# A decoder layer on one core: the self-attention stage rebuilt around stacked queries, two heads per score product and values in column quarters

## The reference

```python
x = x + self_attn(layernorm(x))      # 32 heads of 16, ONE key and value head shared by all
x = x + cross_attn(layernorm(x), ctx)# 32 heads of 128, 8 key/value heads, rotary positions, mask
x = x + ffn(layernorm(x))            # silu(x Wg) * (x Wu), then Wd; inner size 1376

# self_attn
q = (h @ Wq).reshape(b, s, 32, 16);  k, v = split(h @ Wkv)         # k, v: [b, s, 16]
scores = einsum("bqhd,bkd->bhqk", q, k) / 4 + slope[h] * (pos_k - pos_q)
attn = softmax(where(causal, scores, -inf));  out = einsum("bhqk,bkd->bqhd", attn, v) @ Wo
```

## Time and profile before

| | before |
|---|---|
| median of 3 runs | 1018.83 us (1015.87 to 1019.94) |
| profiled execution | 1015.36 us, of it 1013.5 us from the first to the last instruction (span) |
| TensorE busy | 985.4 us (97%) |
| VectorE, ScalarE, GpSimd busy | 589.1, 429.1, 382.0 us |
| granted TensorE clock, mean | 0.995 of full speed |
| self stage | from 0 to 234.5 us of the span |

### The profile page before, as it was taken

How to read it: one execution, slowest core, us unless ns; L and a number is a source line. 1 busy time by engine, 2 the same in 40 slices (tenths; PEclk the granted TensorE clock), 3 DMA queues, 4 the chain that set the end, 5 groups by cost and what they waited for, 6 DMA issues and landing times. The chain is left out here.

```text
span 1013.5 us, 15742 instructions
## 1 busy us (share of the span) xinstructions
PE 985.4 (97%) x5128; PEld 808.2 (80%) x5128; DVE 589.1 (58%) x973; ACT 429.1 (42%) x1239; POOL 382.0 (38%) x375
## 2 busy tenths in 40 slices
PE   5999999989999999999999999999999989999998
PEld 3877777877888888888888888888888768888787
DVE  3856566635776676666666767667666773343100
ACT  2777676751433533523533533533432543333100
POOL 6422222163652642652642633634623422222200
PEclk9999999989999999999999999999999999999999
DMA  6000000211120210210210200210300012122001
GB/s 202 13 11 11 11 10 10 63 52 52 32 63 11 55 50 0 72 31 0 72 31 0 72 31 0 73 30 11 82 1 0 33 32 68 67 71 74 10 32 42
DMA packets 41538, 40.17 MB, mean 40 GB/s; under 512 B 3104, under 2 KB 28832, under 8 KB 41504
## 3 DMA queue, kind: packets, MB, share of 16 engines
q1 hardware_dynamic: 41120, 38.68, 12.7%
q0 software_dynamic: 384, 1.05, 0.3%
HBM read 37.62 MB, written 2.10 MB: 39 GB/s over the span
## 5 line engine op out<-in xcount | busy, mean ns | idle before, releaser
L624 PE MATMUL bank<-cross_wo_hl,cross_outT_hl 128*128 128x512 f32 x768 | 191.7, 398 | 1.0 <-POOL cross_wo_hl L618 0.6
L624 PE MATMUL bank<-hsT_hl,cross_wqkv_hl 128*128 128x512 f32 x768 | 188.2, 394 | 0.0
L624 PEld LDWEIGHTS bank<-cross_wo_hl,cross_outT_hl 128*128 128x128 f32 x768 | 143.1, 188 | 35.5 <-POOL cross_wo_hl L618 1.6
L624 PEld LDWEIGHTS bank<-hsT_hl,cross_wqkv_hl 128*128 128x128 f32 x768 | 141.9, 188 | 29.3
L937 ACT ACTIVATE cross_scores<-cross_scores,cross_negmax 128x128 f32<-128x128 f32 x256 | 99.8, 391 | 127.1 <-DVE cross_negmax L875 127.1
L797 POOL TENSOR_TENSOR cross_qT<-rotated,rotated_other_half 128x512 f32<-128x512 f32 x64 | 82.8, 1293 | 161.9 <-DVE rotated_other_half L839 161.9
L624 PE MATMUL bank<-hsT_hl,ff_gate_upT_hl 128*128 128x512 f32 (+1 forms) x528 | 120.4, 390 | 2.7 <-DVE ff_gate_upT_hl L1139 2.7
L624 PEld LDWEIGHTS bank<-hsT_hl,ff_gate_upT_hl 128*128 128x128 f32 (+1 forms) x528 | 97.7, 185 | 25.0 <-DVE ff_gate_upT_hl L1139 3.1
L947 ACT CAST cross_outT_hl<-bank 128x512 fp32r<-128x512 f32 x64 | 37.1, 579 | 143.4 <-PE bank L624 142.5
L837 DVE TENSOR_TENSOR rotated<-bank,cosT 128x512 f32<-128x512 f32 x80 | 55.2, 690 | 71.4 <-PE bank L624 71.3
L624 PE MATMUL bank<-ctxT_hl,cross_wqkv_hl 128*128 128x512 f32 x384 | 94.3, 394 | 1.1 <-PEq L74 1.1
(11 more groups left out here) (117 smaller groups left out, 1535.6 us busy)
## 6 DMA issues: line engine op xcount, KB each, us to landing
staged_rows<-in_wq SPq DMA_DIRECT2D x32, 256.0 KB, 2.8
staged_rows<-in_wo SPq DMA_DIRECT2D x32, 256.0 KB, 2.7
staged_rows<-in_wg SPq DMA_DIRECT2D x11, 256.0 KB, 2.5
staged_rows<-in_wu SPq DMA_DIRECT2D x11, 256.0 KB, 2.6
staged_rows<-in_wd SPq DMA_DIRECT2D x11, 256.0 KB, 2.7
ctx_tok<-in_ctx SPq DMA_DIRECT2D x8, 256.0 KB, 2.6
staged_rows<-in_wk SPq DMA_DIRECT2D x8, 256.0 KB, 3.0
staged_rows<-in_wv SPq DMA_DIRECT2D x8, 256.0 KB, 3.0
```

Of the source, the lines that this page charges most:

```text
L624: i = nc.tensor.matmul(out, stationary[:, a], moving[:, b], start=(first and k == 0), stop=(last and k == 2))
```

## The change

Only the self stage, its constants and the layout of its inputs change; the cross stage and the feed-forward keep their instructions.

- Normalised rows are kept for four sequences at a time, transposed and split into high and low parts in `hsT` (which the cross stage uses later). Queries of four sequences are made at once, transposed from the start (512 columns are 4 x 128 tokens), with float32r products and split weights; so are keys and values. Four sequences are done before the first scores, four while sequences 2 and 3 run.
- `stack_queries` copies the queries of one sequence with 12 DMAs from SBUF to SBUF: for each of four groups of 32 rows (two heads), the high part goes to rows 0 to 31 and 32 to 63 of `qT`, the low part to rows 64 to 95. Rows 96 to 127 hold the slopes and slopes times positions, loaded once. `qT` has room for two sequences. `kexp` holds for all sequences, in the same rows, the high, low and high parts of the keys of two heads side by side, and positions. One score product then gives two heads with their bias: a step is two products of 256 columns, each started and ended by itself.
- VectorE adds only the causal mask (one 128 x 128 table). ScalarE exponentiates in place with the accumulator. VectorE takes the reciprocal of the row sums, GpSimd multiplies the probabilities by it.
- Values: after four steps (16 heads), four float32 products take 32 columns of a table with the values between zeros as the stationary operand and 512 columns of transposed probabilities as the moving one, and write the four 32-row quarters of one bank; a second group of four adds the other 16 heads. The result is already transposed for the output product, which is made with float32r products of split parts.
- The context comes in already transposed (laid out on the host) and is split by ScalarE and GpSimd in sequences 4 and 5. The rotary tables are gathered at the start and transposed in sequence 0.
- Side work uses three banks (`MB`), in an order that `before_attention` and `steps_in` write out.

```diff
+BANKS = 3
+SLOT_S = 4
+SLOT_PT = 6
+RINGS = 2
+GROUPS_OF_ROWS = ((0, 0), (1, 0), (2, 1))
+Q_DMAS = 16 * QUAD * len(GROUPS_OF_ROWS)
+def before_attention():
+    return ([("ln", c, (0,)) for c in range(HALF)] + [("q", c, (0, 1, 2, 3)) for c in range(HALF)]
+            + [("kv", 0, (0, 1, 2, 3)), ("vt", 0, (0,))])
+def steps_in(b, s):
+    front, back = (0, 1), (2, 3)
+    own = {
+        (0, 0): [("tab", 0, (0,))], (0, 1): [("tab", 1, (0,))], (0, 2): [("tab", 2, (0,))], (0, 3): [("tab", 3, (0,))],
+        (0, 4): [("ln", 4, (0,))], (0, 5): [("ln", 5, (0,))], (0, 6): [("ln", 6, (0,))], (0, 7): [("ln", 7, (0,))],
+        (1, 0): [("kv", 1, front)], (1, 1): [("kv", 1, back)], (1, 3): [("vt", 1, (0,))],
+        (2, 1): [("q", 4, front)], (2, 2): [("q", 4, back)], (2, 3): [("q", 5, front)], (2, 4): [("q", 5, back), ("ln", 8, (0,))],
+        (2, 7): [("q", 6, front)], (3, 0): [("q", 6, back)], (3, 1): [("q", 7, front)], (3, 2): [("q", 7, back)],
+    }.get((b, s), [])
+    if b >= 1 and s in (5, 6):
+        own = own + [("out", b - 1, front if s == 5 else back)]
+    if 3 <= b < SEQS and s == 3:
+        own = own + [("ln", SEQS + b - 2, (0,))]
+    return own
...
+            def load_q(b, quarters=range(QUAD)):
+                sp.wait_ge(sem["bank_read"], use_of("q", HALF * (b // HALF) + HALF - 1) + 1)
+                if b >= RINGS:
+                    sp.wait_ge(sem["scores1"], STEPS * (b - RINGS + 1))
+                for r in quarters:
+                    stack_queries(sp, sem, qT, q_hl, b, r)
...
+            def probs(n):
+                pool.wait_ge(sem["rinv1"], n + 1)
+                nc.gpsimd.tensor_tensor(S[:, n % SLOT_S], S[:, n % SLOT_S], rinv[:, n % SLOT_S, :].unsqueeze(2).to_broadcast([P, QUAD, P]),
+                                        ALU.mult).then_inc(sem["probs1"], 1)
...
+                    dve.wait_ge(sem["scores1"], n + 1)
+                    if n >= SLOT_S:
+                        dve.wait_ge(sem["probs_transposed1"], n - SLOT_S + 1)
+                    nc.vector.tensor_tensor(S[:, n % SLOT_S], SC[n % 2][:].rearrange("p (h k) -> p h k", h=QUAD),
+                                            causal[:].unsqueeze(1).to_broadcast([P, QUAD, P]), ALU.add).then_inc(sem["biased1"], 1)
+                    dve.wait_ge(sem["biased1"], n + 1)
+                    nc.vector.tensor_reduce(negmax[:, n % SLOT_S, :], S[:, n % SLOT_S], AX.X, ALU.max, negate=True).then_inc(sem["max1"], 1)
+                    if n >= 1:
+                        dve.wait_ge(sem["exp1"], n)
+                        nc.vector.reciprocal(rinv[:, (n - 1) % SLOT_S, :], rowsum[:, (n - 1) % SLOT_S, :]).then_inc(sem["rinv1"], 1)
+                    for kind, i in ended_in(b, s):
+                        read_bank(kind, i)
...
+                    for kind, i in ended_in(b, s):
+                        high(kind, i)
+                    if b >= 1 and s == 4:
+                        attnT_high(b - 1)
+                    if n >= 3:
+                        probsT(n - 3)
+                    act.wait_ge(sem["max1"], n + 1)
+                    for j in range(QUAD):
+                        e = nc.scalar.activation(S[:, n % SLOT_S, j, :], S[:, n % SLOT_S, j, :], ACT.Exp, bias=negmax[:, n % SLOT_S, j:j + 1],
+                                                 accum_out=rowsum[:, n % SLOT_S, j:j + 1])
+                    e.then_inc(sem["exp1"], 1)
...
+            def scores(n):
+                b, s = n // STEPS, n % STEPS
+                if s == 0:
+                    pe.wait_ge(sem[f"q_loaded{b % RINGS}"], Q_DMAS * (b // RINGS + 1))
...
+                if n >= 2:
+                    pe.wait_ge(sem["biased1"], n - 1)
+                for k in range(2):
+                    e = nc.tensor.matmul(SC[n % 2][:, k * 2 * P:(k + 1) * 2 * P], qT[:, b % RINGS, 2 * s + k, :], kexp[:, b, :], start=True, stop=True)
+                e.then_inc(sem["scores1"], 1)
+            def values(w):
+                b, second = w // 2, w % 2
+                pe.wait_ge(sem["probsT1"], QUAD * w + QUAD)
...
+                for j in range(QUAD):
+                    e = nc.tensor.matmul(OB[32 * j:32 * j + 32, :], v[:, b, 0:32] if second else v[:, b, 16:48],
+                                         PT[:, (QUAD * w + j) % SLOT_PT], start=not second, stop=bool(second))
+                e.then_inc(sem["pv1"], 1)
+            for kind, i, tiles in before_attention():
+                step(kind, i, tiles)
+            scores(0)
+            for b in range(SEQS):
                 for s in range(STEPS):
                     n = STEPS * b + s
+                    if n + 1 < STEPS * SEQS:
+                        scores(n + 1)
+                    if n >= 3:
+                        transposes(n - 3)
+                    if n >= 7 and n % QUAD == 3:
+                        values(n // QUAD - 1)
+                    for kind, i, tiles in steps_in(b, s):
+                        step(kind, i, tiles)
+            for n in range(STEPS * SEQS - 3, STEPS * SEQS):
+                transposes(n)
+            values(2 * SEQS - 1)
+            step("out", SEQS - 1, (0, 1, 2, 3))
+def stack_queries(queue, sem, qT, q_hl, b, r):
+    at = (b % HALF) * P
+    for group, part in GROUPS_OF_ROWS:
+        queue.dma_start(qT[32 * group:32 * group + 32, b % RINGS].rearrange("p (c r) k -> p c r k", r=QUAD)[:, :, r, :].bitcast(F32),
+                        q_hl[32 * r:32 * r + 32, part, :, at:at + P].bitcast(F32)).then_inc(sem[f"q_loaded{b % RINGS}"], 16)
```

More of the change, by code:

```diff
@@ new lines, in last_of, with bank_uses, use_of, highs_before @@
+def last_of(kind):
+    return 3 if kind in ("q", "kv", "out") else 0
+def bank_uses():
+    uses = [(kind, i) for kind, i, tiles in before_attention()]
+    for b in range(SEQS + 1):
+        for s in range(STEPS):
+            uses += [(kind, i) for kind, i, tiles in steps_in(b, s) if last_of(kind) in tiles]
+    return uses
+USES = bank_uses()
+def use_of(kind, i):
+    return USES.index((kind, i))
+def highs_before(u):
+    return sum(1 for kind, i in USES[:u] if kind != "out")
+def ended_in(b, s):
+    if s == 0:
+        b, s = b - 1, STEPS
+    return [(kind, i) for kind, i, tiles in steps_in(b, s - 1) if last_of(kind) in tiles] if b >= 0 else []
@@ new lines, in _ @@
+            load_q(0, (0, 1))
+            load_q(1)
+            load_q(2)
+            load_q(3)
+            load_ctx(0)
+            load_ctx(1)
+            load_q(4)
+            for j in range(2, 5):
+                load_ctx(j)
+            load_q(5)
+            for j in range(5, 8):
+                load_ctx(j)
+            for j in range(PIECES):
+                if j == 0:
+                    sp.wait_ge(sem["wo1_low"], QUAD)
+                if j == SLOTS:
+                    load_q(6)
+                    load_q(7)
@@ L279, in body @@
+            read_bank("ln", 3)
+            dve.wait_ge(sem["wkv1_high"], 1)
+            nc.vector.tensor_tensor(wkv_hl[:, 1], wkv[:], wkv_hl[:, 0].bitcast(F32), ALU.subtract).then_inc(sem["wkv1_low"], 1)
+            for c in range(HALF):
+                read_bank("q", c)
+            read_bank("kv", 0)
+            read_bank("vt", 0)
+            dve.wait_ge(sem["causal_loaded"], 16)
+            for b in range(SEQS):
                 for s in range(STEPS):
                     n = STEPS * b + s
-                    if s == 3 and since(b, 1):
-                        normalise(b - 1, 1)
@@ new lines, in _ @@
+            for t, done in ((0, "wq1_first"), (2, "wq1_second")):
+                act.dma_start(wq[:, t:t + 2, :], io["wq1"].rearrange("(t p) n -> p t n", p=P)[:, t:t + 2, :]).then_inc(sem[done], 16)
+            for t in range(KT):
+                if t % 2 == 0:
+                    high("ln", t)
+                    high("ln", t + 1)
+                act.wait_ge(sem["wq1_first" if t < 2 else "wq1_second"], 16)
+                nc.scalar.copy(wq_hl[:, 0, t, :], wq[:, t, :]).then_inc(sem["wq1_high"], 1)
@@ L375, in body @@
+            act.wait_ge(sem["wkv1_loaded"], 16)
+            nc.scalar.copy(wkv_hl[:, 0], wkv[:]).then_inc(sem["wkv1_high"], 1)
+            for c in range(HALF):
+                high("q", c)
+            act.wait_ge(sem["bank_read"], use_of("q", HALF - 1) + 1)
+            for r in (2, 3):
+                stack_queries(act, sem, qT, q_hl, 0, r)
+            high("kv", 0)
+            high("vt", 0)
+            for b in range(SEQS):
                 for s in range(STEPS):
                     n = STEPS * b + s
-                    if s == 1 and scores and since(b, 1):
-                        copy_qT(b, 1)
@@ L468, in hs_transposes @@
[L468 to L484 removed]
+                    i = nc.tensor.transpose(bank[:, t * width:(t + 1) * width], src[:, t * P:(t + 1) * P], ident[0:width, 0:width])
```

731 lines of the change are left out of this document (310 added, 421 removed).

## The result

The change made the kernel slower by about one per cent. It takes 1028.28 us (median of 4 runs, 1027.03 to 1029.58), against 1017.35 us for the kernel before on the same chip (4 runs): a ratio of 1.0106, 95% interval 1.0076 to 1.0135. The forecast was 1000 us, with a range of 985 to 1018, and 0.12 for slower. The profiled execution took 1027.03 us, its span 1024.9 us.

A forecast was written before the change was run, and what follows sets the result against it. TensorE alone was taken to bound the self stage, ScalarE after the change. 40.2 + 158 + 4, a 12.5 us tail and 2.3 for a cold start came out 17.4 us below before: 1000 us, range 985 to 1018.

The forecast's parts named there:

- the paragraph on the transfers: Self stage: twelve 64 KB query DMAs a sequence take 7.5 us, start some 18 us ahead and are mostly hidden.
- The rival that bore its name: Query transfers: each of twelve takes its 2.4 us alone, 29 us a sequence, bounding the stage (1070 us); chance 0.03.
- first exponential: Start of the self stage: ScalarE's first exponential at 40.2 us, against 22.38 before, giving away 17.8 us.
- from there to the end of the last one: Self stage's 64 steps: ScalarE's work 158 us plus 4 us of stalls, last exponential at 202 us.
- tail, to the cross stage's first product: Behind the last exponential: nothing overlaps, 12.5 us with hops, so the cross stage starts at 214.8 us.
- the cross stage's first 12 products: Start of the cross stage: these products start at the lower clock and cost 2.3 us more.
- a plain step: Self stage, four heads on ScalarE: exponential set 1.65 us plus bank copy 0.48 us, 2.13 us in all.
- Quarters: Value products: four writing different 32-row quarters overlap, 1 us a group, against 3.6 one after another.
- The rival of the quarters: Value products run one after another, TensorE takes 17.7 us a plain sequence, kernel 1015 us; chance 0.27.
- The clock's rival: TensorE's clock stays low in sequences 1 to 3, 28 us more in all, kernel 1028 us; chance 0.09.

The follow-up runs named there:

- both edits: Kernel after the change, with query transfers of sequences 5 to 7 earlier in SyncE's list and the sixth weight piece's copy later in ScalarE's: 1002.40 us.
- the kernel with one quarter: Kernel with both edits, but all four value products of a group added into the bank's first 32 rows (output not the attention's): 1018.58 us.
- the dense start: Kernel with both edits, plus 28 unused float32r products between the first key product and the first value transpose: 1001.96 us.

## Why the prediction was wrong

**The step that failed** is the paragraph on the transfers: that they start when the ring comes free, "some 18 us ahead, so they are hidden, except for sequence 4 [...] and the first", and that "what is queued behind them on SyncE are context and piece loads that are needed a sequence later". It looked at what stands behind the transfers in the list and not at what stands ahead. SyncE works its list off in order and a wait holds up all behind it. Ahead of sequence 5 stood loads that wait for a split in the last steps of sequence 4, so the lead (18 us in the forecast, 22 in the trace) was gone before the first issue. TensorE then waited 9.63 and 8.22 us where the forecast had nothing. With the list in the other order the step is true, and the cross stage starts 20.5 us earlier.

**The rival that bore its name** was about something else. It asked whether transfers land one after another (29 us a sequence) and answered rightly that they don't: twelve take 7.7 to 8.0 us to issue, and the last lands 2.0 us later. That they could start late had no rival and no share of the chances, and the range's upper end came from the quarters.

**The sum by its terms**, for the kernel after the change and for the one with both edits:

| term | forecast | after | both edits |
|---|---|---|---|
| first exponential | 40.2 | 44.48 | 45.41 |
| from there to the end of the last one | 162 | 183.35 | 162.56 |
| tail, to the cross stage's first product | 12.5 | 18.11 | 12.47 |
| the cross stage's first 12 products | +2.3 | none (3.00 us, 2.98 before) | none (3.01) |

- *Start, 4.3 us late*, mis-sized. The query products started at 18.21 us instead of 16, behind GpSimd's split of the weights; the six issues on ScalarE took 4.00 us instead of 2.8, 0.67 each, where the earlier trace rows had 0.46 for a load from HBM; and the five key copies took 3.1 instead of 2.6.
- *Attention, 162*: right once the waits are out, but with luck, since its parts compensate: a plain step has a pitch of 2.02 us instead of 2.13, and sequence 1 took 24.5 where the sum of its parts had 20.5. The trace shows where much of that went, and it is an order again: TensorE's list has six key products (L641) ahead of transposes that ScalarE needs. They waited for the split of the last normalised rows and then ran at a granted clock of 0.50, and ScalarE stood idle (both edits):

```profile
68.06 2.84 PE L641 MATMUL bank<-hsT_hl,self_wkv_hl 128*96 128x512 f32 x6 [2.43 <-DVE hsT_hl L308]
71.91 0.59 ACT L422 COPY self_probsT<-bank 128x512 f32<-128x512 f32 x1 [2.69 <-PE bank L549]
```

In the kernel with one quarter the clock is 1.00 there, the same products take 1.61 us, and that step 3.26 us instead of 4.85. No run moved these products alone.

- *Tail, 12.5*: right to 0.03 us with the sixth piece's copy out of the way, part of it luck (the output product took 4.66 instead of 5.4, transposes and values 0.34 more than priced); 5.6 too little with the copy. The step that said "Behind it, nothing overlaps" listed the tail's own chain and left out a copy that ScalarE's order puts into it. It is the same mistake as the list's: an instruction with a late releaser ahead of one on the path.
- *The cross stage's cold start, 2.3*: wrong. Its first 12 products follow twelve output products, have a granted clock of 1.00 and take as long as before.
- *Quarters*: the lower end was right and 1 us a group was a little short; 1.33 on the mean, 1.06 in the groups at the upper clock level (eight records in the row at 210.15). The Trainium skill ("TensorE: Matmul & The Clock Gate", Packing small matmuls) gives 2.38 times for three column tiles; here four gave 63.7/21.3 = 3.0 times on the mean and 3.62/1.06 = 3.4 at the upper level. The Trainium skill's rule that a change of tiling mode drains the array ("TensorEngine Tiling (Array Packing)", Key Properties) shows in no row: the group of 1.06 us starts at 210.15 and the next product of 128 columns at 211.14. By an estimate from these starts, a drain behind the group costs no more than some 0.1 us, the 0.99 between them less the 0.90 of one float32 product.
- *The rival of the quarters* was priced at 15 us and cost 16.2 when it was made to happen, but not where it was priced: of its 8.7 us in sequences 2 and 3 the profiles show 6.5 (by the first exponential of each sequence), they show 7.8 in sequences 4 to 6, and the tail, priced at 3 more, did not grow (11.99 us). So the number is right in part by luck.
- *The clock's rival*: the granted clock was indeed low (0.84 from 60 to 200 us after the change, 0.72 in sequence 0 with both edits). In sequence 0 it cost nothing, as the dense start showed, and from 200 to 228 us, at 0.88, ScalarE was busy 27.77 of 28 us all the same. It cost something where the path runs through TensorE: 2.4 us in the tail, and in the first step of sequence 1 up to 1.6 us by the comparison above, which no run made alone.

With both edits the kernel takes 1002.40 us, 2.4 above the forecast, and 13.2 less than the kernel before beside it, where the forecast's sum had 17.4. So the change in TensorE's work, which most of the prediction was about, was read rightly in the main, and the prediction was lost on the order of two lists: some 20 us on SyncE's, some 5 on ScalarE's.

## What to carry to other kernels

When a change puts transfers on a queue that has a hand-written order, read the list upwards from each transfer: the last wait ahead of it, and what releases that, sets when it can start, however early its own buffer is free. The same holds for a copy with a late source in an engine's order ahead of the path's last instructions. And before a low clock is blamed or cured, see which engine sets the pace of that stretch: raising it from 0.71 to 0.87 in sequence 0 was worth nothing, where ScalarE and VectorE did, and from 0.59 to 1.00 in the tail 2.4 us, where the path ran through TensorE.

## What the chip showed that was not expected

The 64 KB copies within SBUF took 0.56 to 0.71 us to issue (7.68 to 8.04 for twelve on SyncE, 4.00 and 4.28 for six on ScalarE, 3.37 for six on GpSimd), where the one 64 KB load from HBM of the earlier trace rows took 0.43, though they landed sooner, 2.0 us after the issue against that load's 2.4. By an estimate from these numbers, issuing all 96 takes some 60 us, nearly all of it on SyncE.
